# Flamingo block with a gated mixture of experts: group 0's first gates spread by TensorE, its weights split in three turns, group 1's second norm later, constant products in TensorE's waits

## The chip, the cores and the metric

The kernel runs on one core of a Trainium2 chip. The metric is the device time of a launch in microseconds; the runs of the kernel before gave 799.54, 800.27 and 800.44, median 800.27. Engines: TensorE (PE, its weight loads PEld), VectorE (DVE), ScalarE (ACT), GpSimd (POOL) and SyncE (SP), which issues nearly all DMAs. All times below are microseconds from the start of the profiled span unless marked ns.

## The reference

64 sequences of 128 tokens with 128 channels. Cut to what is computed:

```
x = x + tanh(g_xattn) * cross_attention(ctx, layernorm(x))        # 77 context tokens a sequence
h = layernorm(x)
logits = (h/|h|) @ (sim/|sim|) - sigmoid(gates)                   # 16 experts
w = softmax over active experts (those with logits > 0, or the top 2 if there is none)
q, k, v = sum_e w[:, e] * (h @ proj_m[e])       for m in q, k, v  # 16 experts each
o = softmax(q k^T / sqrt(128)) v                                  # within a sequence
x = x + tanh(g_ffn) * sum_e w[:, e] * (o @ o_proj[e])
```

## The kernel before

The 64 sequences are 16 groups of four, so a group has 512 tokens, one full row of a PSUM bank. TensorE's main work is a pass per group with 16 steps (experts). In `experts(i, s)` (L1380) expert s of group i adds its products to the three accumulators acc_q, acc_k, acc_v: for each of the three, high weights by high half of the data, low weights by high half, high weights by low half, nine matmuls of 128x512 in half precision. Each number is split in a high and a low float16 part so that the sum is nearly as exact as float32.

The data of a step are made by a chain over three engines: DVE multiplies the normalized tokens x2T_p by the gate of the expert, spread over all partitions (`zq_scale`, L1145, writes zq_full); ACT rounds this to float16 (`zq_high`, L743); POOL subtracts to get the low half (`zq_low`, L658). They run LEAD = 4 steps ahead of TensorE. The spread gates (wq_bc) come through DRAM: DVE transposes the gates to w_blk, SP writes them to w_rows and reads each row back to all 128 partitions (`weight_rows` L468, `spread_q` L476), two experts a transfer.

Beside a pass run, at fixed steps, the small stages of the neighbouring groups: cross attention of group i+2, second norm (`second_stats`, `second_rstd`, `x2_norm`) and gates (`gate_logits`, `gate_mask`, `gate_softmax`) of group i+1, attention and output products of group i-1 (`y_pair`, L1409). There is no scheduler: every engine's order is written out in its `head()` and in `body(i)`, which runs over the steps s, and semaphores join the engines. `late(i)` shifts the gate steps of pass 0.

The head does groups 0 and 1 up to their first norms and loads the projections into `stage`. The projections must be scaled to float16: `weight_max` (L1020) takes the largest entry of each, `gather_max` (L1366) and `spread_max` (L1371) bring it to all partitions through TensorE, `weight_scales` makes the factors, then `weight_high` (ACT, L737) and `weight_low` (DVE, L1068) split a whole projection of 2048 columns per instruction. For q, k, v this is in the head; o_proj follows in pass 0 (`MAX_AT`, `SHARE_AT`, `HIGH_AT`, `LOW_AT` name the steps). `first_expert` (L1396 to L1401) is expert 0 of group 0 in an order of its own. `keep_busy(n)` (L1560) is n matmuls of the identity by itself, whose result is never read.

## Time and profile before

| | us |
|---|---|
| median of three runs (lowest, highest) | 800.27 (799.54, 800.44) |
| profiled execution | 799.99 |
| its span | 798.1 |
| first expert's first matmul | 43.21 |
| start of expert 8 of pass 0 | 63.80 |
| TensorE busy in the span | 776.1 |

The span is what the rows are read from; 1.9 of the profiled execution's time lie around it. A busy TensorE is not TensorE at its peak: matmuls overlap, so what the start times of successive instructions say counts. A row of the timeline gives start, duration, engine, line, operation, the tile written and the tiles read, and in brackets the idle time before it with what ended it.

### The profile page before, as it was taken

Reading aid. Unit: us, or ns where it says so; the run is one execution under the profiler, and the core shown is the slowest. Engines: PE = TensorE matmul, PEld = TensorE weight load, DVE = VectorE, ACT = ScalarE, POOL = GpSimd, SP = SyncE. Lnnn points to the kernel's source line nnn. Section 1 sums busy time; section 2 is a strip of 40 time slices with the busy share of each in tenths; the row PEclk is TensorE's granted clock in tenths of the full one; section 3 lists DMA queues with packets and bytes.
Section 4 is the critical chain, followed back from the end, with each engine's and each line's share of the span. In section 5 each row is a group of like instructions: output and inputs, shape, how many; then the busy total and the mean of one; then the engine's idle time right before and its main releaser. Section 6 shows DMA issues by size and latency. Waiting matters only on the chain.

```text
span 798.1 us, 13995 instructions
## 1 busy us (share of the span) xinstructions
PE 776.1 (97%) x3999; PEld 418.1 (52%) x3999; DVE 607.2 (76%) x2037; ACT 433.8 (54%) x1129; POOL 483.0 (61%) x703
## 2 busy tenths in 40 slices
PE   7489999999999999999999999999999999999998
PEld 6445545555455555545555554555555455544444
DVE  2977787878787787778777787877878786775648
ACT  5554645556555655655565565456556555544445
POOL 3276657674746757474675747567574755765534
PEclk9789999999999999999999999999999999999999
DMA  6564476563655636365563636546364654543100
GB/s 192 136 216 159 162 219 174 169 209 94 209 161 164 189 106 204 97 210 167 151 191 106 202 109 209 166 150 186 101 207 116 208 160 139 163 135 116 53 14 28
DMA packets 97476, 122.57 MB, mean 154 GB/s; under 512 B 14611, under 2 KB 69111, under 8 KB 97399
## 3 DMA queue, kind: packets, MB, share of 16 engines
q1 hardware_dynamic: 96679, 121.59, 49.6%
q8 instruction: 32, 0.52, 0.3%
q14 instruction: 45, 0.37, 0.1%
q10 hardware_dynamic: 720, 0.08, 0.1%
HBM read 97.32 MB, written 24.31 MB: 152 GB/s over the span
## 4 chain that ended last, share of the span: by engine, by line
PE 88%; DVE 5%; DMA 2%; POOL 1%; ACT 1%; issue 1%; SPq 0%; DVEq 0%; ACTq 0%; POOLq 0%
PE acc_q L1380 20%; PE acc_k L1380 20%; PE acc_v L1380 20%; PE y L1409 9%; PE oT_p L1409 9%; PE m L1489 2%; PE m L1553 2%; DVE x_all L1175 1%; PE oT_p L1641 1%; PE m L1480 1%; PE m L1539 1%; DMA stage<-in_L_ffn_q_proj_dram 1%; PE m L1469 1%; POOL zq L658 1%; PE m L1529 1%
## 5 line engine op out<-in xcount | busy, mean ns | idle before, releaser
L658 POOL TENSOR_TENSOR zq<-zq_full,zq 128x512 f16<-128x512 f32 x256 | 297.8, 1170 | 222.4 <-ACT zq L743 222.2
L743 ACT ACTIVATE zq<-zq_full 128x512 f16<-128x512 f32 x256 | 160.1, 636 | 224.1 <-DVE zq_full L1145 224.0
L1175 DVE SCALAR_TENSOR_TENSOR x_all<-y,w_out,x_all 128x128 f32<-128x128 f32 x356 | 122.2, 343 | 96.1 <-issue 69.5
L1380 PE MATMUL acc_q<-zq,w_hi 128*128 128x512 f16 x510 | 193.3, 379 | 1.0 <-POOL zq L658 1.0
L1380 PE MATMUL acc_k<-zq,w_hi 128*128 128x512 f16 x510 | 193.2, 379 | 0.0
L1380 PE MATMUL acc_v<-zq,w_hi 128*128 128x512 f16 x510 | 193.2, 379 | 0.0
L1145 DVE TENSOR_TENSOR zq_full<-wq_bc,x2T_p 128x512 f32<-128x512 f32 x256 | 167.8, 668 | 2.5 <-DMA wq_bc<-w_rows 1.7
L1175 DVE SCALAR_TENSOR_TENSOR x_all<-oT_p,w_out,x_all 128x128 f32<-128x128 f32 x356 | 121.5, 341 | 0.0
L673 POOL TENSOR_TENSOR x_all<-stage,x_all 128x128 f32<-128x128 f32 x240 | 100.4, 456 | 19.8 <-DVE x_all L1175 13.3
L1380 PE MATMUL acc_q<-zq,w_lo 128*128 128x512 f16 x255 | 96.6, 379 | 0.0
L1380 PE MATMUL acc_v<-zq,w_lo 128*128 128x512 f16 x255 | 96.6, 379 | 0.0
L1380 PE MATMUL acc_k<-zq,w_lo 128*128 128x512 f16 x255 | 96.6, 379 | 0.0
L1409 PE MATMUL y<-w_hi,oT 128*128 128x512 f16 x236 | 89.5, 379 | 1.5 <-ACT oT L975 1.3
L1409 PE MATMUL oT_p<-w_hi,oT 128*128 128x512 f16 x236 | 89.4, 379 | 0.0
L1380 PEld LDWEIGHTS acc_v<-zq,w_hi 128*128 128x128 f16 x510 | 53.7, 105 | 53.3
L1380 PEld LDWEIGHTS acc_q<-zq,w_hi 128*128 128x128 f16 x510 | 51.8, 102 | 53.7 <-POOL zq L658 2.2
L1380 PEld LDWEIGHTS acc_k<-zq,w_hi 128*128 128x128 f16 x510 | 49.8, 98 | 53.3
L770 ACT ACTIVATE stage<-oT_p,w_out 128x128 f32<-128x128 f32 x116 | 33.1, 368 | 69.8 <-PE oT_p L1409 45.6
L1409 PE MATMUL oT_p<-w_lo,oT 128*128 128x512 f16 x118 | 44.7, 379 | 0.0
L1409 PE MATMUL y<-w_lo,oT 128*128 128x512 f16 x118 | 44.7, 379 | 0.0
L1380 PEld LDWEIGHTS acc_k<-zq,w_lo 128*128 128x128 f16 x255 | 26.8, 105 | 26.7
L1380 PEld LDWEIGHTS acc_v<-zq,w_lo 128*128 128x128 f16 x255 | 24.9, 98 | 26.7
(253 smaller groups left out, 1091.4 us busy)
## 6 DMA issues: line engine op xcount, KB each, us to landing
wq_bc<-w_rows SPq DMA_DIRECT2D x128, 512.0 KB, 4.5
blk_rows<-stage SPq DMA_DIRECT2D x26, 256.0 KB, 2.7
stage<-blk_rows SPq DMA_DIRECT2D x104, 64.0 KB, 2.0
blk_rows<-v_blk SPq DMA_DIRECT2D x15, 256.0 KB, 2.0
v_mix<-blk_rows SPq DMA_DIRECT2D x60, 64.0 KB, 2.9
blk_rows<-pc_blk SPq DMA_DIRECT2D x15, 256.0 KB, 4.1
pcT<-blk_rows SPq DMA_DIRECT2D x60, 64.0 KB, 2.0
out_dram<-x_all SPq DMA_DIRECT2D x15, 256.0 KB, 6.7
```

The costliest lines, as they stand in the source:

```text
L658: nc.gpsimd.tensor_tensor(zq[:, 1, e % Z_SLOTS, :], zq_full[:, e % F_SLOTS, :], zq[:, 0, e % Z_SLOTS, :], ALU.subtract).then_inc(zq_lo_poo ...
L673: nc.gpsimd.tensor_tensor(total, y_sc[:, n // 2 % 2, b, j, :], total, ALU.add).then_inc(y_pool_added, 1)
L743: nc.scalar.activation(zq[:, 0, e % Z_SLOTS, :], zq_full[:, e % F_SLOTS, :], ACT.Copy).then_inc(zq_hi_done, 1)
L770: last = nc.scalar.activation(dst, bank[:, tok(j)], ACT.Copy, scale=w_out[:, g % 2, e, b0 + b:b0 + b + 1])
L1145: nc.vector.tensor_tensor(zq_full[:, e % F_SLOTS, :], wq_bc[:, e // 2 % W_SLOTS, e % 2], x2T_p[:], ALU.mult).then_inc(zq_full_done, 1)
L1175: nc.vector.scalar_tensor_tensor(out=rows(x_all, g, b0 + b), in0=bank[:, tok(j)], scalar=w_out[:, g % 2, e, b0 + b:b0 + b + 1], in1=rows(x ...
L1380: last = nc.tensor.matmul(acc[m][:], w[:, m, s, :], zq[:, half, s % Z_SLOTS, :], start=(s == 0 and n == 0), stop=(s == E - 1 and n == 2))
L1409: last = nc.tensor.matmul(bank[:], oT[:, g % 2, half, tok(b)], w[:, O, QUAD * k:QUAD * (k + 1), :].rearrange("p e c -> p (e c)"), start=(n ...
L1469: last = nc.tensor.matmul(m0[:, b * E:(b + 1) * E], x2T[:, tok(b)], sn[:], start=True, stop=True)
L1480: last = nc.tensor.matmul(m1[:, b * S:(b + 1) * S], xnT[:, tok(b)], kxT[:, ctx_slot(g1), b * S:(b + 1) * S], start=True, stop=True)
L1489: done = nc.tensor.matmul(m1[:, tok(b)], qT[:, tok(b)], kT[:, tok(b)], start=True, stop=True)
L1553: last = nc.tensor.matmul(m1[:, tok(b)], pxT[:, tok(b)], vx[:, ctx_slot(g), tok(b)], start=True, stop=True)
```

## The change

1. **First gates by TensorE.** `gate_diagonal(e)` on DVE multiplies the identity by the gates of expert e, four times side by side (128x512, float32), and `gate_spread(e)` on TensorE multiplies a matrix of ones by it: every partition gets the gates of the 512 tokens, in PSUM. This is done for experts 0 and 1 of group 0 (`BY_PE = 2`); the products `zq_scale(0, 0)` and `(0, 1)` read PSUM and x2T, and SP's first transfer of that group's spread gates is left out.
2. **Weights in three turns.** `weight_high` and `weight_low` of q, k, v take a part each time, experts 0 to 3, 4 to 9, 10 to 15 (`PARTS`): the first in the head, the second in the head and at step 0, the third at steps 1 to 4 of pass 0. `experts` waits for the second part at step 4 and for the third at step 10.
3. **Order of the head and of pass 0.** The q projection is loaded before the extra context, x of group 1 before v; group 0's gates come before the weight scales; `att_product(1)`, `x1_add(1)`, `second_stats(1)`, `second_rstd(1)`, `x2_norm(1)` and `first_stats(2)` move from the head into pass 0; `GATES_LATE = 3` puts group 1's second norm and gates two steps later than before; the steps of o_proj's largest entry, its sharing, and its split are each one or two later.
4. **`oT_high(0)`** stands ahead of the step's `zq_high` in pass 1 instead of behind it.
5. **`keep_busy`** stands at ten more places of TensorE's head, before its waits.

```diff
+BY_PE = 2
+PARTS = ((0, 4), (4, 10), (10, 16))
+GATES_LATE = 3
-            return 1 if i == 0 else 0
+            return GATES_LATE if i == 0 else 0
-        MAX_AT, SHARE_AT = (0, 2), ((0, 4), (0, 7))
-        HIGH_AT = (0, 9)
-        LOW_AT = (0, 11)
+        MAX_AT, SHARE_AT = (0, 4), ((0, 5), (0, 8))
+        HIGH_AT = (0, 10)
+        LOW_AT = (0, 12)
...
                 sp.wait_ge(kq_in, 16 * 2)
+                load_weights(Q, q_proj)
                 sp.dma_start(zq_full[0:S, 0:PRE]...   # extra context
-                load_weights(Q, q_proj)
                 load_weights(K, k_proj)
+                load_x(1)
                 load_weights(V, v_proj)
-                load_x(1)
...
                 # POOL, pass 0
+                    if i == 0 and s == 2:
+                        second_rstd(1)
...
+                    if i == 0 and s == 3:
+                        first_rstd(2)
...
                 # ACT, pass 0 and 1
+                    if i == 1 and s == Y_FIRST:
+                        oT_high(0)
                     for g, e in zq_at(i, s):
                         zq_high(g, e)
...
+                    if i == 0 and s == 3:
+                        x2_norm(1)
+                    if i == 0 and s in (1, 2, 3):
+                        weight_high((Q, K, V)[s - 1], 2)
...
+            def gate_diagonal(e):
+                wait(dve, w_ready, 1)
+                nc.vector.tensor_tensor(wq_bc[:, 0, e].rearrange("p (b t) -> p b t", b=G),
+                                        ident[:].unsqueeze(1).broadcast_to([P, G, P]),
+                                        w_new[:, 0, e].unsqueeze(2).broadcast_to([P, G, P]),
+                                        ALU.mult).then_inc(w_diag_done, 1)
...
                 # DVE, head (tail of it)
+                gate_softmax(0)
+                gate_diagonal(0)
                 weight_scales(0)
+                gate_diagonal(1)
                 x_sum(1)
                 zq_scale(0, 0)
+                weight_low(Q)
                 zq_scale(0, 1)
+                weight_low(K)
                 weight_low(V)
+                weight_low(Q, 1)
                 zq_scale(0, 2)
                 zq_scale(0, 3)
+                weight_low(K, 1)
...
+                    if i == 0 and s == 0:
+                        weight_low(V, 1)
+                    if i == 0 and s == 1:
+                        x1_add(1)
+                        second_stats(1)
+                    if i == 0 and s == 2:
+                        first_stats(2)
+                    if i == 0 and s in (2, 3, 4):
+                        weight_low((Q, K, V)[s - 2], 2)
...
+            def gate_spread(e):
+                pe.wait_ge(w_diag_done, e + 1)
+                pe.wait_ge(logit_read, 1)
+                nc.tensor.matmul(SPREAD_BANKS[e][:], ones[:], wq_bc[:, 0, e], start=True,
+                                 stop=True).then_inc(w_spread_ps, 1)
...
                 # TensorE, end of the head
+                keep_busy(8)
+                gate_spread(0)
                 px_transpose(1)
-                att_product(1)
+                keep_busy(2)
+                gate_spread(1)
+                keep_busy(3)
```

TensorE around step 4 and 5 of pass 0. `m<-ident,x` is group 1's transposition after its second norm, `y<-ident,wmax` is `gather_max(1)` for o_proj, `m<-sn,x2T` are group 1's gate logits. Before:

```order
L1500 MATMUL m<-ident,x 128x128 x3
L1380 MATMUL acc_q<-zq,w_hi 128x512 [waits zq_lo_pool]
L1380 MATMUL acc_q<-zq,w_lo 128x512
L1380 MATMUL acc_q<-zq,w_hi 128x512
L1380 MATMUL acc_k<-zq,w_hi 128x512
L1380 MATMUL acc_k<-zq,w_lo 128x512
L1380 MATMUL acc_k<-zq,w_hi 128x512
L1380 MATMUL acc_v<-zq,w_hi 128x512
L1380 MATMUL acc_v<-zq,w_lo 128x512
L1380 MATMUL acc_v<-zq,w_hi 128x512
L1366 MATMUL y<-ident,wmax 4x128 [waits prep_dve,wmax_done]
```

and with the change:

```order
L1439 MATMUL acc_v<-zq,w_hi 128x512
L1561 MATMUL m<-ident,x 128x128 [waits xnT_sb,zq_full_done,logit_read,x2_done]
L1561 MATMUL m<-ident,x 128x128 x3
L1421 MATMUL y<-ident,wmax 4x128 [waits prep_dve,wmax_done]
L1439 MATMUL acc_q<-zq,w_hi 128x512 [waits zq_lo_pool]
```

Both now stand between experts 5 and 6; they were behind experts 3 and 4, a whole expert between them.

DVE around `weight_max(O)`, which is `wmax<-stage`, the instruction that `gather_max(1)` waits for. Before, its neighbours are the products of experts 6 and 7:

```order
L1007 BN_AGGR mv<-bn 128x2 x3
L1145 TENSOR_TENSOR zq_full<-wq_bc,x2T_p 128x512 [waits zq_lo_pool,wq_in2]
L1145 TENSOR_TENSOR zq_full<-wq_bc,x2T_p 128x512 [waits zq_lo_pool]
L1145 TENSOR_TENSOR zq_full<-wq_bc,x2T_p 128x512 [waits zq_lo_pool,wq_in3]
L1020 TENSOR_REDUCE wmax<-stage 128x1 [waits proj_in3]
```

and with the change, where w_lo are the third parts for q, k and v:

```order
L1037 BN_AGGR mv<-bn 128x2 x3
L1098 SCALAR_TENSOR_TENSOR w_lo<-stage,w_up,w_hi 128x768 [waits hi_done0]
L1190 TENSOR_TENSOR zq_full<-wq_bc,x2T_p 128x512 [waits zq_lo_pool]
L1098 SCALAR_TENSOR_TENSOR w_lo<-stage,w_up,w_hi 128x768 [waits hi_done1]
L1190 TENSOR_TENSOR zq_full<-wq_bc,x2T_p 128x512 [waits zq_lo_pool,wq_in0]
L1098 SCALAR_TENSOR_TENSOR w_lo<-stage,w_up,w_hi 128x768 [waits hi_done2]
L1020 TENSOR_REDUCE wmax<-stage 128x1 [waits proj_in3]
```

It stood behind seven products (experts 0 to 6) and now stands behind nine, and behind three more pieces of the weights.

ACT in pass 1 at step 8. Before:

```order
L820 ACTIVATE gate_e<-gate_arg 128x64 [waits gate_arg_done]
L743 ACTIVATE zq<-zq_full 128x512 [waits zq_used,zq_full_done] x3
L975 ACTIVATE oT<-oT_p 128x512 [waits oT_ps]
L850 ACTIVATE px,sum_x<-m,nmax_x 128x77 [waits rsum_x_done,pxT_ps,xmax_done]
```

and with the change:

```order
L837 ACTIVATE gate_e<-gate_arg 128x64 [waits gate_arg_done]
L760 ACTIVATE zq<-zq_full 128x512 [waits zq_used,zq_full_done] x2
L899 ACTIVATE oT<-oT_p 128x512 [waits oT_ps]
L760 ACTIVATE zq<-zq_full 128x512 [waits zq_used,zq_full_done]
L867 ACTIVATE px,sum_x<-m,nmax_x 128x77 [waits rsum_x_done,pxT_ps,xmax_done]
```

The rounding of group 0's attention output (oT) goes one product forward.

## Rows read from the trace of the kernel before

**Rows 1.** The page: busy time of each engine, with its share and instructions.
```profile
PE 776.1 (97%) x3999; PEld 418.1 (52%) x3999; DVE 607.2 (76%) x2037; ACT 433.8 (54%) x1129; POOL 483.0 (61%) x703
```

**Rows 2.** TensorE's waits from 57 to the end: total, times, longest.
```profile
PE y L1409 <- ACT oT L975: 1.3, 2, 1.0
```

**Rows 3.** Stretches: length, busy PE, PEld, DVE, ACT, POOL, PEclk, DMA share, GB/s.
```profile
28.00:32.90 4.90, 0.00 (x0) 0.00 (x0) 4.35 (x34) 3.56 (x6) 1.71 (x4) 0.57 0.04 11
43.20:46.90 3.70, 3.53 (x9) 0.88 (x9) 3.67 (x8) 0.90 (x2) 3.70 (x2) 0.65 0.66 264
54.43:63.80 9.37, 9.37 (x51) 5.11 (x51) 7.04 (x25) 4.84 (x11) 7.78 (x9) 1.00 0.53 170
102.55:103.74 1.19, 0.16 (x1) 0.03 (x1) 0.11 (x1) 1.19 (x4) 0.97 (x2) 1.00 1.05 278
```

**Rows 4.** Timeline, TensorE, pass 0 and 1.
```profile
56.38 0.27 PE L1366 MATMUL y<-ident,wmax 128*4 128x128 f32 x1
63.80 0.39 PE L1380 MATMUL acc_q<-zq,w_hi 128*128 128x512 f16 x1
...
100.60 0.38 PE L1380 MATMUL acc_q<-zq,w_hi 128*128 128x512 f16 x1
102.33 0.38 PE L1380 MATMUL acc_v<-zq,w_hi 128*128 128x512 f16 x1
103.74 0.38 PE L1409 MATMUL y<-w_hi,oT 128*128 128x512 f16 x1 [1.03 <-ACT oT L975]
104.38 0.39 PE L1409 MATMUL y<-w_hi,oT 128*128 128x512 f16 x1
```

**Rows 5.** Timeline, DVE, from group 0's gates to o_proj's largest entry.
```profile
34.33 2.31 DVE L1068 SCALAR_TENSOR_TENSOR w_lo<-stage,w_up,w_hi 128x2048 f16<-128x2048 f32 x1
...
41.36 1.28 DVE L1145 TENSOR_TENSOR zq_full<-wq_bc,x2T_p 128x512 f32<-128x512 f32 x2 [1.71 <-DMA wq_bc<-w_rows]
...
45.42 1.12 DVE L1218 SCALAR_TENSOR_TENSOR x_all<-m,rsum_x,x_all 128x128 f32<-128x128 f32 x4
...
47.78 0.65 DVE L1145 TENSOR_TENSOR zq_full<-wq_bc,x2T_p 128x512 f32<-128x512 f32 x1
...
51.31 2.28 DVE L1020 TENSOR_REDUCE wmax<-stage 128x1 f32<-128x2048 f32 x1
```

**Rows 6.** Timeline, DVE and POOL, where both want SBUF at once.
```profile
29.88 0.23 DVE L1088 TENSOR_TENSOR logit<-logit,sig 128x64 f32<-128x64 f32 x1
...
43.03 5.11 POOL L658 TENSOR_TENSOR zq<-zq_full,zq 128x512 f16<-128x512 f32 x3 [12.47 <-ACT zq L743]
...
57.15 4.51 POOL L658 TENSOR_TENSOR zq<-zq_full,zq 128x512 f16<-128x512 f32 x4
...
59.38 1.23 DVE L1088 TENSOR_TENSOR logit<-logit,sig 128x64 f32<-128x64 f32 x1
```

**Rows 7.** Timeline, ACT.
```profile
40.45 1.99 ACT L737 ACTIVATE w_hi<-stage,w_up 128x2048 f16<-128x2048 f32 x1
...
51.36 1.63 ACT L781 ACTIVATE x<-x_all,shift,rstd 128x128 f32<-128x128 f32 x4
...
102.48 0.63 ACT L743 ACTIVATE zq<-zq_full 128x512 f16<-128x512 f32 x1 [0.75 <-DVE zq_full L1145]
103.02 0.58 ACT L975 ACTIVATE oT<-oT_p 128x512 f16<-128x512 f32 x1
```

**Rows 8.** Timeline, POOL: first and last instruction of `second_rstd(1)` and of `second_norm(1)`.
```profile
48.23 0.23 POOL L641 TENSOR_SCALAR shift<-mv 128x4 f32<-128x4 f32 x1
...
49.95 0.20 POOL L646 TENSOR_TENSOR shift<-shift,rstd 128x4 f32<-128x4 f32 x1
...
55.58 0.23 POOL L650 TENSOR_SCALAR norm<-mv 128x4 f32<-128x4 f32 x1
...
57.00 0.20 POOL L654 TENSOR_TENSOR norm<-norm,rstd 128x4 f32<-128x4 f32 x1
```

**Rows 9.** Timeline, TensorE: a float32 matmul of 308 columns in the head.
```profile
18.66 0.69 PE L1529 MATMUL y<-ctxT,m_kq 128*128 128x308 f32 x2
```

More of the change, by code:

```diff
@@ L411, in vx_bank, with split_part @@
             return (acc[V], oT_p, acc[K])[g - 1] if 1 <= g <= PRE else m0
+        SPREAD_BANKS = (m0, oT_p)
+        def split_part(t, m, part):
+            experts = slice(*PARTS[part]) if m < O else slice(0, E)
+            return t[:, m, experts].rearrange("p e h -> p (e h)")
         def ctx_slot(g):
@@ L507, in head @@
                 weight_rows(0)
-                for j in range(W_SLOTS):
+                for j in range(BY_PE // 2, W_SLOTS):
                     spread_q(0, j)
@@ L682, in head @@
                 first_rstd(1)
-                for e in range(LEAD - 1):
+                for e in range(LEAD):
                     zq_low(0, e)
-                second_rstd(1)
-                zq_low(0, LEAD - 1)
-                first_rstd(2)
             def body(i):
@@ L877, in pxT_out, with oT_high @@
                                          px_mix[:].rearrange("p i b n -> p b i n"), ACT.Copy).then_inc(pxT_sb, 1)
+            def oT_high(g):
+                wait(act, oT_ps, g + 1)
+                wait(act, y_ps, PAIRS_Y * (g - 1))
+                nc.scalar.activation(oT[:, g % 2, 0, :], oT_p[:], ACT.Copy).then_inc(oT_hi_done, 1)
             def head():
@@ L904, in head @@
                 xnT_out(1)
-                x2T_move(0)
+                x_exps(1)
+                weight_high(Q)
                 weight_high(K)
-                x_exps(1)
+                zq_high(0, 0)
+                weight_high(V)
                 pxT_out(1)
-                weight_high(V)
-                for e in range(LEAD):
-                    zq_high(0, e)
+                zq_high(0, 1)
+                weight_high(Q, 1)
+                weight_high(K, 1)
+                zq_high(0, 2)
+                weight_high(V, 1)
+                zq_high(0, 3)
             def body(i):
@@ L932, in body @@
                         y_scale(gd, 7, banks=(0,))
-                    if s == (3 if i == 0 else 0) and has(g1):
+                    if s == (4 if i == 0 else 0) and has(g1):
                         x_norm(g1)
@@ L971, in body @@
                         kxT_out(g1)
-                    if s == Y_FIRST and has(gc):
-                        wait(act, oT_ps, gc + 1)
-                        wait(act, y_ps, PAIRS_Y * (gc - 1))
-                        nc.scalar.activation(oT[:, gc % 2, 0, :], oT_p[:], ACT.Copy).then_inc(oT_hi_done, 1)
+                    if s == Y_FIRST and i > 1 and has(gc):
+                        oT_high(gc)
                     if s == 10 - sooner(i) and has(g1):
@@ L1376, in experts @@
                 for m in (Q, K, V):
+                    for part, (first, _) in enumerate(PARTS):
+                        if (i, s) == (0, first):
+                            pe.wait_ge(hi_done[m], part + 1)
+                            pe.wait_ge(lo_done[m], part + 1)
                     if s == 0:
@@ L1506, in xn_transpose @@
                     wait(pe, kxT_sb, 2)
-                wait(pe, logit_read, cap(g))
+                if g == 2:
+                    wait(pe, x1_done, 2)
                 for b in range(G):
-                    last = nc.tensor.transpose((acc[Q] if g == 1 else m0)[:, tok(b)], xn[:, b, :], ident[:])
+                    last = nc.tensor.transpose((m0, acc[Q], m1)[g][:, tok(b)], xn[:, b, :], ident[:])
                 last.then_inc(xnT_ps, 1)
@@ L1574, in head @@
                 vx_product(0)
-                for g in range(1, PRE + 1):
-                    ctx_transpose(g)
-                px_transpose(0)
-                kx_product(1)
-                att_product(0)
-                vx_product(1)
-                for g in range(2, PRE + 1):
+                ctx_transpose(1)
+                px_transpose(0)
+                for g in range(2, PRE + 1):
+                    ctx_transpose(g)
+                att_product(0)
+                for g in range(1, PRE + 1):
                     kx_product(g)
@@ L1618, in body @@
                         scores(gc, i)
+                    if i == 0 and s == 0:
+                        att_product(1)
                     if s == 2 + late(i) and g2 < X2_HEAD:
```

77 lines of the change are left out of this document (43 added, 34 removed).

## Prediction

> **What bounds the kernel now.** I read the page's busy times first: TensorE is busy for 776.1 of 798.1 [rows 1]. Then TensorE's waits: from 57 on there is one of weight, 1.3 before the first output products, of which 1.0 in one piece [rows 2]. So the end is set by how early TensorE gets into its unbroken stream and by that one wait; nothing else in 740 us is for sale. Third, stretches: from 54.43 TensorE is busy all of 9.37 at clock 1.00 (2.4 GHz), while it stood still from 28.0 to 32.9 and did the first expert at a mean clock of 0.65, that is, mostly at 1.2 GHz [rows 3]. Last the timelines, for what each wait in pass 0 hangs on.
>
> I measure the change at one mark: the start of expert 8 of pass 0, 63.80 before [rows 4]. Behind it both kernels have the same work left but for one small matmul (`spread_max(1)`, now behind expert 8), 0.1. All times are on the scale of the profiled execution; its time is 799.99, 0.28 under the median of the runs shown.
>
> **The change part by part: the front of the head.** Loads are reordered. The q projection starts earlier, but the extra context now comes behind it, and group 0's score transposition stands behind a transposition that waits for that context. DVE loses the weight scales (moved behind the gates) and gains group 1's row maxima ahead of w_blk, the point at which DVE began the low weights, 34.33 [rows 5]. I add these up to w_blk at 34.0; the order of the two loads could make it one earlier or nearly one later.
>
> **First products.** From 34.0 on DVE does a diagonal (512 columns, like a product, which has 1.28/2 = 0.64 [rows 5]), the scales (five operations of under 0.23 [rows 6], 0.85), a second diagonal, and a short reciprocal: 36.2. The spread is a float32 matmul of 512 columns, which the trace doesn't have; from 0.69 for 308 columns [rows 9] it is 1.15 by columns, under that if a fixed part is in it, and twice that if the clock is at half: 1.0 to 2.3, and I take 1.0, since the constant products now fill the waits. The first spread is hidden under the scales; the second ends at 37.6, so the products of experts 0 and 1 start at 36.2 and 37.6, where they started at 41.4 and 42.0, behind a transfer [rows 5]. Expert 2 still needs that transfer: 41.36 - 34.33 = 7.0 after w_blk, 41.0.
>
> **First experts.** The first part of the weights is 512 columns: ACT 1.99/4 = 0.5 and a little [rows 7], DVE 2.31/4 = 0.6 and a little [rows 5]; I take 0.5 and 0.65, and 0.75 and 0.9 for 768 columns. TensorE starts its first expert at 38.2 instead of 43.2. An expert is 1.94: eight steps from 100.60 to 102.33 make 0.216, times nine [rows 4]. With `att_product(1)` (0.9) and waits of 1.8 for the third low part and 0.4 and less for products 2 and 3, experts 4 and 5 run from 49.2 to 53.1. In the kernel before, expert 4 began at 54.43 [rows 3]. Up to here 5 us are won.
>
> **What takes them back.** Behind expert 5 stand two waits. `x2_transpose(1)` needs the second norm of group 1: DVE does `x1_add(1)` and its statistics (45.42 to 47.78, 2.35 [rows 5]) at 46.7 to 49.1, POOL's reciprocal root takes 48.23 to 50.15, 1.9 [rows 8], so 51.3, and ACT's norm 1.63 [rows 7] stands behind the product of expert 7: 53.0 to 54.7. The transposition ends at 55.1. Then `gather_max(1)` needs the largest entry of o_proj, and that is DVE's backlog. Its work from 34.0 to that point: diagonals 1.3, scales 0.85, nine products at 0.62, 5.6, the low weights in three pieces of 0.65 and six of 0.9, 7.4, `x1_add` and its statistics 2.35, the first statistics of group 2 another 1.2, the maximum 2.2 [rows 5], small ones 0.1: 20.9, so 54.9 if DVE never waits. The kernel before was done at 53.59, with two products less, larger pieces and no diagonals.
>
> It will wait. DVE's operations with both inputs in SBUF and POOL's subtractions exclude each other here: 64 columns take 0.23 on a free POOL and 1.23 beside subtractions, and POOL's three subtractions at 43.03 take 5.11, where four take 4.51 at 57.15, because a low weight was running [rows 6]. In the kernel before only the last low weight met a subtraction. Now eight of the nine pieces come after POOL has begun. Placing them one by one, DVE waits 0.35 at k's first piece, 1.05 at v's, 0.45 at v's second, 0.4 at k's third; and 1.1 at v's third, whose high half stands on ACT behind the second norm (54.7). With 0.4 for the second spread that is 3.75: 58.7. The bounds are no wait for POOL, 2.3 less, and a whole subtraction (4.51/4 = 1.13 [rows 6]) at each of the eight, 5 more than I take.
>
> This is where a page speaks: the Trainium skill, SBUF — State Buffer, section "Who interferes with whom", says that a VectorE instruction with two SBUF inputs and a GpSimd one that reads SBUF take a shared port for the whole instruction, whichever comes first. The rows agree. By it the low weights in small pieces cost no less port time, only more meetings.
>
> So expert 6 starts at 58.85, expert 7 behind the transposition of group 2's norm (0.44), with the logits in it (0.5), and expert 8 at 63.7; before it was 63.80. A second chain ends at nearly the same place, so that a quicker DVE alone doesn't help much: POOL does `second_norm(1)` (55.58 to 57.20, 1.6 [rows 8]) and then `first_rstd(2)` (1.9) ahead of ACT's norm of group 2, which ends at 60.0, and TensorE needs that before expert 7, at 60.8. With the matmul still to do the head is worth 0.0, the 5 us gone into the wait at `gather_max(1)`.
>
> **Pass 1.** The wait before the first output products goes: TensorE is ready at 102.33 + 0.22 = 102.55 and starts at 103.74, busy for 0.16 of the 1.19 between [rows 3]; the third product waits again until 104.38, 0.21 late [rows 4]. ACT did the product of expert 12 first (102.48), then oT, 0.58 [rows 7]. Turned round, oT starts after the product before, at 101.7, and is in time. Next late is `oT_low` on DVE, still behind its product: it would end at 103.1 to 103.4 and hold the third matmul for up to 0.4. Gain 1.19 + 0.21 - 0.4 = 1.0.
>
> **Others.** Group 1's gates now follow on the logits in expert 7, so that they come two steps nearer to their use. From 63.8 DVE has some 25 small operations of 0.23 and less [rows 6] and two products, 5.7, so 69.5; 7.0 for the way through DRAM as for group 0, 76.5; then product, rounding and subtraction, 2.4, with `weight_low(O)` in between, 2.3 by the first low weight [rows 5]: 81.2. TensorE needs it at 63.8 plus eight experts and 2.1 of small matmuls, 81.4. So this is only just hidden, and each us that the gates slip further costs up to 1. The constant products lie in waits: nothing. The second and third weight waits at steps 4 and 10 are met 3 and more earlier.
>
> Sum: 799.99 - 0.0 - 1.0 = 799.0.
>
> **The rivals.**
> - *An earlier, looser head* (faster). The q load lands sooner and carries DVE's chain with it by 1.0, which reaches the mark whole, since both waits behind expert 5 hang on it; port waits half as long give 0.5 more. 799.0 - 1.5 = 797.5. For it: the mark moves one for one with w_blk. Against it: the context behind the q load.
> - *The clock falls in the new wait* (no change). TensorE stands from 55.1 to 58.8, 3.7, after another 1.6. In a stop of 4.9 the clock was at half for most of it and stayed so into the first experts [rows 3]. Half of 2.7 us of experts at half speed is 1.35: 800.35. Decides if the stop stays over some 3. The Trainium skill, TensorE: Matmul & The Clock Gate, section "Why this matters for your kernels", warns of idle gaps between bursts for this reason; the constant products stand in the head alone, not here.
> - *The spreads run at half clock* (slower; also: the constant products don't do what they say). Then the second spread ends at 40.6, as group 1's transposition and the constant products ahead of it are slow too; the second product is 3.0 late, of which DVE's later waits absorb 1.2. The rest, 1.8, reaches `gather_max(1)`, and the clock is lost there as well: 799.0 + 1.8 + 1.35 = 802.15. It decides from w_blk plus 4.5 for the second product. For it: clock 0.57 from 28.0 to 32.9 [rows 3]. Against it: the waits there are now filled.
>
> **How the numbers follow.** Forecast 0.42, earlier head 0.25, clock in the wait 0.19, half-clock spreads 0.14. The forecast's own range is 798.2 to 799.9. 0.2% is 1.6, about what a measurement of this kernel can tell from no change: faster is under 798.7, slower over 801.9. Faster: all but a little of the second case and a third of the forecast's, 0.24 + 0.14 = 0.38. Slower: most of the last and the tail of the third, 0.13. Same 0.49. The range 796.6 to 802.0 leaves out one tenth on either side: below, w_blk one earlier and no port waits; above, the last case.
>
> **What would show it.** w_blk near 34.0; the first product before 37 and the first expert near 38; low weights of 128x768 that last 1.0 and more instead of 0.9; TensorE idle for about 3.7 before `y<-ident,wmax`, ended by DVE's maximum at 58.7; PEclk 1.00 from 28 to 55; expert 8 near 63.7; no wait on oT in pass 1. It is wrong if the matmul of o_proj's maximum doesn't wait, which would mean that DVE isn't behind (then expert 8 comes up to 1 earlier), or if TensorE waits at the first expert of pass 1 for its low half.

## The result and the profile after

The changed kernel took 807.45 us (median of 4 runs, 806.79 to 808.93), the kernel before 800.36 (4 runs, 799.54 to 800.63): ratio 1.0093, 95% interval 1.0075 to 1.0110. It is slower by 7.1; the forecast was 799.0, with 802.0 as the range's upper end. The profiled run was the slowest of the four, 808.93 with a span of 807.1 against 798.1 before, so the traces have 9.0 to explain, 1.9 more than the medians. From the page of the changed kernel, the lines that answer to [rows 1]:

```profile
PE 784.2 (97%) x4055; PEld 424.3 (53%) x4055; DVE 609.4 (76%) x2045; ACT 434.2 (54%) x1135; POOL 483.9 (60%) x703
...
PE   5979989999999999999999999999999999999998
...
PEclk9998999999999999999999999999999999999999
...
PE 86%; DVE 6%; DMA 4%; issue 1%; ACT 1%; SPq 1%; DVEq 0%; ACTq 0%
```

TensorE is busy 8.1 longer with the constant products in it, and the chain of work that ended last now passes more through transfers (DMA 4%, where the kernel before has 2%). Which ones, its list of waits says (what it waited for, total, times, longest), against [rows 2]:

```profile
PE y L1582 <- DMA zq_full<-in_ctx_dram: 3.7, 1, 3.7
PE y L1421 <- DVE wmax L1050: 3.4, 1, 3.4
...
PE oT_p L1721 <- DMA pcT<-blk_rows: 2.9, 1, 2.9
PE acc_q L1439 <- POOL zq L674: 1.5, 2, 1.1
...
PE y L1469 <- ACT oT L899: 0.3, 1, 0.3
```

Three pieces of 2.9 and more: the first (context) and the third (the transposed probabilities of pass 1) were not there before, the second is the wait that the prediction placed. The same list shows the wait on oT down from 1.3 to 0.3. The first in TensorE's timeline (start, duration):

```profile
16.58 0.49 PE L1582 MATMUL y<-ident,zq_full 77*128 77x77 f32 x4 [3.67 <-DMA zq_full<-in_ctx_dram]
...
18.72 2.00 PE L1615 MATMUL m<-vx,pxT 77*128 77x128 f32 x8
```

The eight matrix products at 18.72 take 2.00, where they took 1.16 before: behind the stop TensorE runs at 1.2 GHz. They are group 0's cross attention, which VectorE adds to x on the way to the gates:

```profile
20.75 1.13 DVE L1263 SCALAR_TENSOR_TENSOR x_all<-m,rsum_x,x_all 128x128 f32<-128x128 f32 x4 [4.53 <-PE m L1615]
```

In the kernel before this sum began at 19.02. Stretches of the changed kernel (length, busy, granted clock), three stops and what followed each:

```profile
12.90:16.60 3.70, 0.03 (x2) 1.00 1.08 276
16.60:22.00 5.40, 5.40 (x29) 0.53 0.98 281
28.00:32.90 4.90, 4.77 (x42) 1.00 0.12 32
...
57.20:60.66 3.46, 0.04 (x1) 0.61 0.88 272
60.66:64.90 4.24, 4.24 (x12) 0.52 0.07 22
...
105.40:108.36 2.96, 0.02 (x2) 1.00 0.34 89
108.36:112.50 4.14, 4.14 (x16) 0.59 1.01 294
```

After each of these three stops some 4 to 5 us are at about half (0.52 to 0.59); from 28.0 to 32.9, where the kernel before stood still at 0.57 [rows 3], the clock is full. VectorE's timeline gives the second stop and what stands behind group 1's gates:

```profile
57.40 1.02 DVE L1098 SCALAR_TENSOR_TENSOR w_lo<-stage,w_up,w_hi 128x768 f16<-128x768 f32 x1 [1.08 <-ACT w_hi L754]
58.33 2.28 DVE L1050 TENSOR_REDUCE wmax<-stage 128x1 f32<-128x2048 f32 x1
...
73.75 0.24 DVE L1170 STREAM_TRANSPOSE w_blk<-w_new 128x64 f32<-128x64 f32 x1
...
81.69 0.69 DVE L1190 TENSOR_TENSOR zq_full<-wq_bc,x2T_p 128x512 f32<-128x512 f32 x1 [3.77 <-DMA wq_bc<-w_rows]
82.29 2.34 DVE L1098 SCALAR_TENSOR_TENSOR w_lo<-stage,w_up,w_hi 128x2048 f16<-128x2048 f32 x1
...
91.46 0.71 DVE L1111 STREAM_TRANSPOSE stage<-xn 128x512 f32<-128x512 f32 x1 [1.04 <-ACT xn L821]
```

VectorE stands for 3.77 on the transfer of group 1's gates, and only then does the low half of o_proj and all that leads to group 3's norm, whose block is ready at 92.2. That is 1.2 behind the scores (91.01), where it was 0.8 behind them before (86.12 and 85.28). SyncE's queue in pass 1, of the changed kernel:

```profile
92.20 0.32 SPq L471 DMA_DIRECT2D blk_rows<-stage  x1
...
97.44 2.68 SPq L477 DMA_DIRECT2D stage<-blk_rows  x4
100.17 0.43 SPq L492 DMA_DIRECT2D wq_bc<-w_rows  x1
100.64 0.43 SPq L471 DMA_DIRECT2D blk_rows<-pc_blk  x1
```

and of the kernel before:

```profile
86.12 0.32 SPq L455 DMA_DIRECT2D blk_rows<-stage  x1
...
89.37 1.73 SPq L461 DMA_DIRECT2D stage<-blk_rows  x4
91.14 0.43 SPq L476 DMA_DIRECT2D wq_bc<-w_rows  x1
92.54 0.34 SPq L455 DMA_DIRECT2D blk_rows<-pc_blk  x1
```

In this kernel SyncE waits until a block has landed in DRAM before it fetches it back (the four transfers from blk_rows), and what stands behind that wait in its order stands too. Before, the probabilities' block left as soon as it was ready. Now the norm's block takes 5.2 from issue to landing instead of 3.2, and the probabilities, ready at 98.3, leave at 100.64. TensorE, in the changed kernel:

```profile
108.36 1.34 PE L1721 MATMUL oT_p<-pcT,v_sb 128*128 128x128 f32 x8 [2.94 <-DMA pcT<-blk_rows]
109.49 0.63 PE L1439 MATMUL acc_q<-zq,w_hi 128*128 128x512 f16 x1
...
112.95 0.38 PE L1469 MATMUL y<-w_hi,oT 128*128 128x512 f16 x1
```

The first output product follows its expert at once, so that the wait of [rows 4] is gone, but most of the expert ran at half clock (a product every 0.43 instead of 0.22).

The whole difference, by five marks of the timelines, one profiled execution of each kernel. The rows below the second are the experiments of the next section. The marks: the first w_blk on VectorE; group 2's score transposition on TensorE (behind expert 12 of pass 0); the scores of pass 1; the oT product; the first output product.

| | w_blk | to transp. | to scores | to oT | to output | to end |
|---|---|---|---|---|---|---|
| before | 34.16 | 40.08 | 11.04 | 14.36 | 4.10 | 694.36 |
| changed | 36.35 | 42.13 | 12.53 | 17.35 | 4.59 | 694.15 |
| a1 context first | 33.01 | 41.83 | 12.44 | 16.87 | 4.59 | 694.16 |
| a2 busy gather | 36.85 | 40.15 | 12.91 | 15.49 | 2.91 | 694.19 |
| a3 gather later | 37.80 | 42.64 | 12.22 | 16.78 | 4.52 | 694.24 |
| a4 low half earlier | 37.38 | 42.16 | 12.13 | 15.22 | 2.91 | 694.20 |
| b1 = a1 + a2 | 33.23 | 40.13 | 12.71 | 15.52 | 2.91 | 694.20 |
| b2 = b1 + a4 | 33.50 | 40.14 | 12.12 | 14.92 | 2.91 | 694.21 |
| b3 gates earlier | 33.09 | 42.87 | 11.04 | 14.97 | 2.91 | 694.12 |
| b4 before, oT first | 33.82 | 40.01 | 11.04 | 14.43 | 2.91 | 694.29 |
| c1 gather later, filled | 33.84 | 40.46 | 11.50 | 14.79 | 2.91 | 694.20 |
| c2 pxT first | 33.78 | 40.16 | 11.61 | 15.12 | 2.91 | 694.22 |
| c3 three chains | 33.87 | 38.65 | 11.05 | 15.98 | 2.91 | 694.14 |
| c4 no constants | 34.32 | 41.83 | 12.13 | 14.36 | 2.91 | 694.15 |
| d1 block order | 36.29 | 42.19 | 12.80 | 14.81 | 2.91 | 694.20 |
| d2 = c3 + d1 | 33.67 | 38.66 | 11.05 | 14.65 | 2.91 | 694.16 |
| d3 = c3, gates earlier | 33.04 | 39.62 | 11.04 | 15.95 | 2.91 | 694.24 |

Changed less before, column by column: 2.19 + 2.05 + 1.49 + 2.99 + 0.49 - 0.21 = 9.0. The first column moves from run to run (the five kernels with the q load first lie at 36.3 to 37.8, the ten others with a diagonal at 33.0 to 34.3). So a median and a column of the table can tell different amounts, and where they do, both are given. The second, fifth and last column repeat to about 0.1, the two between to about 0.5, since transfers are in them.

### The profile page after: what moved, and what is told of

Same layout as the page of the kernel before. It is cut to its first block, busy times and chain, and to the rows that moved or that the text cites. A ratio compares the mean times of both kernels' runs of the same rounds, so it can differ in the third digit from the quotient of the medians.

```text
span 807.1 us, 14130 instructions
## 1 busy us (share of the span) xinstructions
PE 784.2 (97%) x4055; PEld 424.3 (53%) x4055; DVE 609.4 (76%) x2045; ACT 434.2 (54%) x1135; POOL 483.9 (60%) x703
## 4 chain that ended last, share of the span: by engine, by line
PE 86%; DVE 6%; DMA 4%; issue 1%; ACT 1%; SPq 1%; DVEq 0%; ACTq 0%
PE acc_k L1439 19%; PE acc_q L1439 19%; PE acc_v L1439 19%; PE oT_p L1469 9%; PE y L1469 9%; PE m L1549 2%; PE m L1615 2%; PE oT_p L1721 2%; DVE x_all L1220 1%; PE m L1601 1%; PE m L1540 1%; DVE zq_full L1190 1%; DMA zq_full<-in_ctx_dram 1%; PE m L1529 1%; PE m L1591 1%
```

## The experiments

**a1**, the load order alone.

```diff
-                load_weights(Q, q_proj)
                 sp.dma_start(zq_full[0:S, 0:PRE]..., c_v[:, G:G * (PRE + 1), :])...
+                load_weights(Q, q_proj)
```

> The changed kernel with one thing undone: the extra context is loaded ahead of the q projection again, as in the kernel before. Theory A: the late head is a late context. TensorE's wait of 3.7 for it (12.9 to 16.6) goes, and with it the half-speed stretch behind it; the first w_blk comes at 34.0 to 34.5 instead of 36.4 (by the end of the softmax on VectorE), expert 8 of pass 0 at 65.4 to 65.7 instead of 67.64, and all that follows is 2.0 to 2.3 earlier: about 805.3 as a median against 807.4. Rival B: the path to w_blk goes over the q projection's maximum on VectorE; then w_blk stays at 36 or comes later, and the time stays at 807.4 or rises.

Measured 804.71 (5 runs, 802.57 to 806.05; ratio to before 1.0048, 1.0029 to 1.0066), 2.7 under the changed kernel. w_blk comes 3.3 earlier, at 33.01; no later column moves by over 0.5. Theory A, and in the trace more than it said. VectorE in a1:

```profile
16.02 2.29 DVE L1049 TENSOR_REDUCE wmax<-stage 128x1 f32<-128x2048 f32 x1 [2.11 <-DMA stage<-in_L_ffn_q_proj_dram]
...
18.50 1.13 DVE L1262 SCALAR_TENSOR_TENSOR x_all<-m,rsum_x,x_all 128x128 f32<-128x128 f32 x4
```

Here the sum that TensorE held up until 20.75 in the changed kernel comes at 18.50, right behind the q projection's maximum, which had waited for its load. So rival B named a path that is real, but only once the context is in time: with the q load first the way to w_blk goes over the context and TensorE, with the context first over the q load and its maximum.

**a2**, constant products in the wait at the gather.

```diff
                     if (i, s) == SHARE_AT[0]:
+                        keep_busy(12)
                         gather_max(1, y0)
```

> The changed kernel with twelve constant products of 128 columns (about 0.22 each, 2.6 in all) ahead of the transposition of the weights' maxima in pass 0, in TensorE's wait of 3.4. Theory A: the clock falls to half because TensorE stands there, and that costs 1.9 of its own: expert 6 begins at 60.9 as now, but the experts behind it run at 1.94 instead of 3.85, expert 8 comes at 65.7 to 66.0 instead of 67.64, and the time is 1.7 to 1.9 less, about 805.6. Rival B: another engine sets the pace behind the wait (the norm of group 2 on ScalarE ends at 62.0, so expert 7 cannot begin before 62.5), and at most 0.5 comes back. Rival C: the gates of group 1 and the transfers behind them set the time in pass 1, and the gain in pass 0 is lost there.

Measured 806.37 (4 runs, 804.26 to 807.55; ratio 1.0081, 1.0064 to 1.0098). That is 1.1 under the changed kernel, less than theory A's 1.7 to 1.9, and the two intervals overlap: the time alone doesn't settle it. The profiled run is the fastest of the four, so what it shows in pass 1 need not be typical. In the trace:

```profile
57.60 2.84 PE L1629 MATMUL y<-ident 128*128 128x128 f32 x24
61.18 0.27 PE L1421 MATMUL y<-ident,wmax 128*4 128x128 f32 x1 [0.74 <-DVE wmax L1050]
```

VectorE's maximum ends where it did against w_blk, expert 6 takes 1.94 instead of 3.84, and the second column is 40.15 instead of 42.13: the clock is worth 2.0 in that column. b1 against a1, the same edit with ten runs, has 1.7 there. Theory A by the trace; B falls, the norm of group 2 is in time for this. Rival C said that pass 1 would take the gain back; b1, below, speaks against it.

**a3**, the gather moved away from the wait.

```diff
-        MAX_AT, SHARE_AT = (0, 4), ((0, 5), (0, 8))
+        MAX_AT, SHARE_AT = (0, 4), ((0, 7), (0, 9))
```

> The changed kernel with the transposition of the weights' maxima moved from behind expert 5 to behind expert 7, and their spread from behind expert 8 to behind expert 9. Theory A (the second chain of the prediction): TensorE starts expert 6 at 57.2 instead of 60.9, but then waits at the transposition of group 2's norm until the norm ends at 62.0, some 2.9, so that only 2 to 3 are won: expert 8 at 64.9 to 65.7, time about 805. Rival B: VectorE's maximum was the only wait; all of 3.4 and the clock's 1.9 come back, expert 8 at 62.4, time about 802.

Measured 807.66 (4 runs, 806.35 to 809.99; the slowest was profiled): nothing won, both expectations too good. TensorE's row, with the wait in brackets:

```profile
63.53 1.12 PE L1571 MATMUL m<-ident,xn 128*128 128x128 f32 x4 [2.89 <-ACT xn L821]
```

The second chain is there, 2.9 of wait in the place of 3.4. The transposition comes 2.6 sooner behind w_blk than in the changed kernel (25.7 against 28.3), but the clock falls as well (0.63 from 63.5 to 72.0) and takes it all back: 42.64.

**a4**, the low half of o_proj in VectorE's wait.

```diff
-        LOW_AT = (0, 12)
+        LOW_AT = (0, 11)
```

> The changed kernel with the low half of o_proj (2.3 on VectorE) moved ahead of the first product of pass 1, into VectorE's wait of 3.8 for the transfer of group 1's gates. Theory A: the low half behind that wait holds up VectorE's queue, ScalarE's and then the transfers: the wait of 0.45 at the first expert of pass 1 goes, the block of group 3's norm leaves 2.1 earlier (90.1 instead of 92.2), so that the probabilities' block no longer stands behind it in the transfer queue (issued by 98 instead of 100.64), TensorE's wait of 2.9 for the transposed probabilities goes and the clock stays full: 4 to 5 less, about 802.8. Rival B: the transfer of the gates itself (74.0 to 81.6) sets pass 1, and the low half only fills a gap: at most 0.6 less, about 806.8.

Measured 805.41 (4 runs, 805.00 to 806.02; ratio 1.0063). Scores to oT 15.22 instead of 17.35, the stop before oT 0.8 instead of 2.9, and the clock holds: 2.91 instead of 4.59. In those columns that is 3.8; the medians differ by 2.0, under A's 4 to 5 and over B's 0.6; w_blk was 1.0 later in that run. Only the place of VectorE's piece was changed, but A's way to the gain is not what the trace shows: the norm's block leaves at 92.51, 0.8 behind the scores instead of 1.2, so 0.4 sooner and not 2.1, and it is fetched 3.2 behind its issue instead of 5.2. Most of the column's gain is that shorter transfer, and why it was shorter stays open (below).

**b1** and **b2**, the edits together (a1 + a2, and a4 on top).

> The changed kernel with the extra context ahead of the q load (a1) and the twelve constant products ahead of the transposition of the maxima (a2). Theory A: the two are independent terms, the late context about 2.7 and the clock about 2.0 at the mark (the first part of group 2's score transposition in TensorE's row came 40.15 behind w_blk with the products, 41.83 to 42.13 without). So that transposition comes 40.2 behind w_blk, level with the kernel before (40.08), and the time is 801.5 to 803.5, still above 800.4 by what the late gates cost in pass 1. Rival B: the waits in pass 1 hang on transfers that started at fixed times, and the two gains do not add: 804.7 as a1.

> b1 with the low half of o_proj ahead of the first product of pass 1 (a4's edit). Theory A: VectorE's queue behind the transfer of the gates is the third term; alone it gave 2.0. Scores to oT product in pass 1: 15.2 instead of about 16.9, and the stop before oT under 1, so that the clock holds; the time is 1.5 to 3 under b1, 799.5 to 801.0. Rival B: b1 has ended the long stop already (with the clock), and this gives at most 0.5.

Measured: b1 800.69 (10 runs, 800.37 to 801.71; ratio 1.0006, 0.9997 to 1.0016), b2 799.53 (10 runs; 0.9988, 0.9979 to 0.9998). b1 is 6.8 under the changed kernel, better than theory A: the stop before oT is down to 1.1 and the clock holds there too. Against a1, the constant products are worth 4.0 in the medians, 1.7 of it in pass 0 and the rest in the shorter stop and the kept clock of pass 1; no run here tells why that stop is shorter with them. b2 has another 1.2, less than A's 1.5 and more than B's 0.5. What is left of the two waits in pass 1 that come from group 1's gates, in b2's list of waits:

```profile
PE m L1614 <- ACT pxT L889: 0.8, 1, 0.8
...
PE oT_p L1720 <- DMA pcT<-blk_rows: 0.5, 1, 0.5
```

**b3**, group 1's gates one expert earlier, on b2.

```diff
-GATES_LATE = 3
+GATES_LATE = 2
...
+                    if i == 0 and s == 2 + late(i):
+                        x2T_out(g2)
                     if s == (4 if i == 0 else 0) and has(g1):
                         x_norm(g1)
...
```

> b2 with group 1's transposition, logits and gates one expert earlier in pass 0 (two behind the kernel before's instead of two and one more: logits in expert 6), and ScalarE's copy of the transposed norm ahead of group 2's norm, since expert 6 needs it. Theory A: the late gates are what is left. The second w_blk comes about 1.5 to 2 earlier, VectorE's wait for the transfer falls from 3.8 to 2 or less, the wait at the attention product of group 2 (0.5 to 1.0, behind the same transfer through ScalarE's queue) goes, and pass 1 has no wait for the transposed probabilities: 1 to 2 under b2, 798.0 to 799.5, under the kernel before. Rival B: VectorE is behind in pass 0 anyway (its maximum of o_proj), so that the gates do not start earlier by more than 0.5 and nothing is won.

Measured 801.56 (10 runs; ratio 1.0016, 1.0003 to 1.0030), 2.0 over b2: neither theory.

```profile
53.34 0.66 PE L1562 MATMUL m<-ident,x 128*128 128x128 f32 x4 [3.24 <-ACT x L797]
...
53.30:60.00 6.70, 6.66 (x36) 0.75 0.57 173
```

The transposition waits 3.2 for a norm that is no earlier against w_blk, and the clock falls for expert 5. But to the scores it takes 11.04, as in the kernel before.

**b4**, the kernel before with the oT move alone.

```diff
+                    if i == 1 and s == Y_FIRST:
+                        oT_high(0)
                     for g, e in zq_at(i, s):
                         zq_high(g, e)
...
```

> The kernel before with one part of the change alone: in pass 1 ScalarE rounds oT ahead of its next rounding of a product. The prediction priced this at 1.0 less. Theory A: the trace of the changed kernel shows the whole wait gone, 1.19 before the first output product, and the third product's 0.21, with no wait at the low half: 1.4 less, 799.0. Rival B: the low half on VectorE is late and holds TensorE at the third product for up to 0.4: 1.0 less, 799.4. Rival C: the product whose rounding is put off delays the next experts: no gain.

Measured 798.92 (10 runs; ratio 0.9985, 0.9976 to 0.9995): 1.3 less. The interval holds both A's 1.4 and B's 1.0; the trace decides for theory A.

```profile
102.21 0.38 PE L1414 MATMUL y<-w_hi,oT 128*128 128x512 f16 x1
...
102.70 0.39 PE L1414 MATMUL y<-w_hi,oT 128*128 128x512 f16 x1
```

The first follows its expert at once, and the third is 0.06 late, where the prediction allowed up to 0.4.

**c1**, **c2**, **c3**, what lies behind the gather, all on b2's edits (c1 and c3 with the constants ahead of group 2's transposition instead of the gather, twelve in c1 and five in c3).

```diff
 c1:
-        MAX_AT, SHARE_AT = (0, 4), ((0, 5), (0, 8))
+        MAX_AT, SHARE_AT = (0, 4), ((0, 7), (0, 9))
 c2, ahead of ScalarE's rounding in step 12:
+                    if i == 0 and s == 12:
+                        pxT_out(g1)
...
 c3, both of these, and on GpSimd:
+                    if i == 0 and s == 3:
+                        first_rstd(2)
                     if s == (3 if i == 0 else 1) and i < 2:
                         second_norm(g2)
 and on ScalarE:
+                    if i == 0 and s == 4:
+                        x2T_out(g2)
                     if s == (4 if i == 0 else 0) and has(g1):
                         x_norm(g1)
...
```

> b2 with the maxima's transposition behind expert 7 (a3's move), and the twelve constant products now ahead of group 2's transposition instead. Theory A: the wait at the gather hides a second wait of nearly the same end, ScalarE's norm of group 2, so that with the clock held the move is worth only 0.6 to 1.0: that transposition comes 25.7 behind w_blk (26.4 in b2), and the time is 798.5 to 799.0. In a3 the same move lost all of it, since the wait of 2.9 was unfilled and the clock fell. Rival B: the norm waits for something that the maximum holds up as well, and nothing is won (799.5).

> b2 with ScalarE's copy of group 2's transposed probabilities ahead of its first rounding of pass 1, which waits for the transfer of group 1's gates. Theory A: TensorE's wait of 0.8 at the attention product of group 2 is that transfer, seen through ScalarE's queue: it goes, and what is late next is the first expert of pass 1, whose gates come with the same transfer: of the 0.8, 0.2 to 0.8 is won, 798.7 to 799.3. Rival B: the first expert of pass 1 waits for the same transfer and takes it all: 799.5.

> c1 and c2 together, with the two other things that hold expert 7: GpSimd takes group 2's reciprocal root ahead of group 1's norm, and ScalarE copies group 1's transposed norm ahead of group 2's norm (five constant products ahead of group 2's transposition). Theory A: three chains end within 2 of each other behind expert 5 (the maximum on VectorE, the norm of group 2 through GpSimd and ScalarE, the copy behind a rounding that waits for VectorE). With all three moved the transposition of group 2 comes 24.0 to 24.7 behind w_blk instead of 26.4, and the time is 1.5 to 2.5 under b2: 797.0 to 798.0, under both kernels. Rival B: a fourth, the roundings and subtractions of experts 8 to 10 behind VectorE's maximum, takes it back: 798.5 to 799.5.

Measured: c1 799.01 (10 runs, 798.17 to 800.82; ratio 0.9985), c2 799.45 (10 runs; 0.9987), c3 797.66 (6 runs, 796.31 to 798.43; ratio 0.9961, 0.9948 to 0.9973). Group 2's transposition comes 25.8 behind w_blk in c1, as said, but 0.5 is lost again in a wait of the spread, the second column is no shorter than b2's, and the medians of the two can't be told apart. c2 takes 0.5 out of the third column, and the median is b2's: too little to tell, rival B as far as one sees. c3 is the one that counts. GpSimd, ScalarE and TensorE in it:

```profile
56.06 0.20 POOL L651 TENSOR_TENSOR shift<-shift,rstd 128x4 f32<-128x4 f32 x1
...
56.30 1.65 ACT L820 ACTIVATE xn<-x_all,shift,rstd 128x128 f32<-128x128 f32 x4 [0.41 <-POOL shift L651]
...
57.99 0.66 PE L1574 MATMUL m<-ident,xn 128*128 128x128 f32 x4 [0.17 <-ACT xn L820]
```

The transposition comes 24.1 behind w_blk and waits for 0.2 only; the second column falls to 38.65, 1.4 under the kernel before. Theory A; how much each of the moved pieces gives was not measured. Its fourth column is 1.1 longer than b2's: the block of the norm took 5.1 there, the probabilities stood behind it on SyncE, and TensorE waited 1.4 for them.

**c4**, b2 without the constant products that the change put into the head. They are eight calls with 26 products (4, 2, 3, 2, 2, 8, 2 and 3). The edit of the first is shown. The expectation's 32 is a miscount, and so are the ten more places that the description of the change names: the changed kernel has ten calls, two of which were there before.

```diff
                 x2_transpose(0)
-                keep_busy(4)
                 pe.wait_ge(vx_sb, PRE)
...
```

> b2 without the eight calls that the change added to the head between group 0's norm and the first expert (32 constant products); those ahead of them and the twelve before the gather stay. Theory A (the rival of the prediction that did not happen): without them the clock falls between w_blk and the first experts as in the kernel before (0.57 from 28 to 33): the spreads take 2.0 each instead of 1.0, the first expert comes 1 to 1.5 later and runs at half speed; VectorE's backlog absorbs most, and the time is 0.5 to 2.5 over b2: 800 to 802. Rival B: TensorE's waits there are short enough without them, or VectorE's backlog absorbs all: 799.5.

Measured 801.78 (10 runs, 800.09 to 803.11; ratio 1.0016, 1.0006 to 1.0025): 2.25 over b2, theory A.

```profile
35.20 2.07 PE L1622 MATMUL m<-wq_bc,ones 128*128 128x512 f32 x2 [2.39 <-DVE wq_bc L1104]
...
37.91 1.92 PE L1622 MATMUL oT_p<-wq_bc,ones 128*128 128x512 f32 x2
...
33.00:37.00 4.00, 1.80 (x2) 0.75 (x3) 3.37 (x14) 2.37 (x10) 0.00 (x0) 0.50 0.06 8
```

At clock 0.50 the spreads take 2.0 each instead of 1.0, w_blk is 0.8 later and the first expert another 1.1.

**d1** and **d2**, SyncE's order in pass 1, on the changed kernel and on c3.

```diff
+                    if s == 3 and i == 1:
+                        wait(sp, pc_blk_done, gc + 1)
+                        blocks_out(2, pc_blk, pc_blk_out)
                     if s == 3 and X_HEAD <= g1 < NG:
                         wait(sp, xn_blk_out, 16 * (g1 - X_HEAD + 1))
...
```

> The changed kernel with one thing moved: in pass 1 SyncE sends the block of group 0's probabilities ahead of fetching the transposed block of group 3's norm, for which it waits 4.6 and spends 2.7 on the issue; nothing is removed. Theory A: TensorE's wait of 2.9 for the transposed probabilities is queueing on SyncE, which lets the block go at 100.64 though it was ready at 98.2: the block leaves 2.4 earlier relative to the scores, the wait falls to 0.5 or so and the clock's 1.7 behind it comes back: 803 to 804.5 against 807.45. Rival B: the transfers themselves are slow there (4.3 for the block, beside the broadcasts of the gates), and the order wins at most 0.5.

> c3 with the same order on SyncE. In c3 the block leaves at 91.73 and was ready at 90.4, and TensorE waits 1.4. Theory A: 1.2 of it goes: 796.2 to 796.8. Rival B (transfers): no change, 797.7.

Measured d1 804.97 (4 runs, 804.67 to 805.91; ratio 1.0060), d2 796.84 (4 runs, 795.49 to 797.87; ratio 0.9954, 0.9938 to 0.9971). SyncE in d1:

```profile
98.57 0.34 SPq L471 DMA_DIRECT2D blk_rows<-pc_blk  x1
99.00 1.82 SPq L477 DMA_DIRECT2D stage<-blk_rows  x4
100.87 0.43 SPq L492 DMA_DIRECT2D wq_bc<-w_rows  x1
101.34 1.85 SPq L477 DMA_DIRECT2D pcT<-blk_rows  x4
```

The probabilities' block leaves when ready and is fetched 2.8 later instead of 4.3, and TensorE waits 0.3 for it instead of 2.9: scores to oT 14.81 instead of 17.35, to the output 2.91 instead of 4.59. Against A's 803 to 804.5 the median is half a microsecond high; B, 0.5 at most, falls. The block also landed sooner once it had left (2.1 instead of 4.3), now ahead of the 512 KB broadcast of wq_bc and no longer behind it, so the order won both the queueing and a quicker transfer, and d1 doesn't part the two. d2's fourth column falls by 1.3, the median by 0.8, with an interval that overlaps c3's. Its median is the lowest of all, 3.3 under the 800.14 of the kernel before that was measured with it, but only the trace sets it apart from c3.

**d3**, b3's question again, on c3 with the wait filled.

```diff
-GATES_LATE = 3
+GATES_LATE = 2
...
+                        if i == 0:
+                            keep_busy(12)
                         x2_transpose(g2)
```

> c3 with group 1's transposition and logits one expert earlier, this time with twelve constant products in the wait ahead of the transposition, so that the clock cannot fall there as it may have in b3. Theory A: the lateness of the gates is itself a term in pass 1, and in b3 it was hidden by the clock: the second w_blk comes 1.5 to 2 earlier (32.0 to 32.5 behind the first, where c3 has 33.98), the wait for the transposed probabilities falls under 0.5, 796 to 797. Rival B: the wait at the earlier transposition (3.2) only moves expert 5, VectorE's products behind it come later, the second w_blk stays at about 34 behind the first and nothing is won or up to 1 is lost.

Measured 798.55 (10 runs; ratio 0.9982): 0.9 over c3. The second w_blk does come 32.4 behind the first (33.98 in c3), but the fourth column stays at 15.95 and the second is 1.0 longer. So with the three chains moved the place of the gates costs nothing more. c3 says the same: its second w_blk comes 4.7 ahead of group 2's score transposition, as in the changed kernel (before: 7.4), and still its third column is the 11.0 of the kernel before. What costs in the fourth column there is the order on SyncE (d2). Theory A had the w_blk right and the time wrong, B the time and not the w_blk.

## Why the prediction was wrong

Most steps of pass 0 came out, measured against w_blk: first expert 4.2 behind it (predicted 4.2), expert 4 14.9 (15.2), o_proj's maximum done 24.3 (24.7), VectorE's wait for v's third part 1.08 (1.1), a spread 1.0 (1.0). With the late context and the clock taken away (b1, b2) the second column is 40.1 against 40.1 before: "the head is worth 0.0" holds, the 5 us are lost at the gather as said, and a3 and c3 show that the second chain was real. The oT move was sized at 1.0 and measured 1.3 (b4); the 0.4 held back for the low half was too much. One bound was added up wrongly without effect: eight whole subtractions of 1.13 instead of the 3.35 of waits taken at those pieces are 5.7 more, not 5. What failed:

- **"I add these up to w_blk at 34.0"**: 36.35, 2.2 late. The text named the context behind the q load and allowed "nearly one". TensorE stood 3.7 for it and then worked at half clock, which the sum had not counted. The early q load did what the first rival said, its maximum began at 13.9 instead of 16.5, but VectorE then stood 4.5 for TensorE. With the order undone w_blk is at 33.0 (a1): the order costs 3.3 in the traces and 2.7 in the medians. Of the 3.3, 2.25 are VectorE's sum (20.75 against 18.50). Most of the rest is in TensorE's order: group 0's transposition for the gates, at 28.09, stood behind late matmuls and the eight constant products that both kernels have there, and began 2.5 behind the start of its norm, 1.7 in a1. Without this order w_blk lies at 33.0 to 34.3, against the 34.0 of the sum.
- **"The clock falls in the new wait"** was a rival at 0.19, priced at 1.35. It happened, at 2.0 (a2; 1.7 from a1 to b1). [Rows 3] showed a stop and a half-speed stretch behind it; this wait was predicted at 3.7 and nothing in the rows said that it was short enough.
- **"this is only just hidden, and each us that the gates slip further costs up to 1."** This is the step that failed worst. Against expert 8, w_blk came 0.6 later than forecast, and the transfer took 7.7 instead of 7.0. At the consumer that the sum had followed, the first expert of pass 1, TensorE waited no more than 0.4 for the low half. Yet pass 1 lost 1.49 + 2.99 and then 1.68 of clock (4.59 against 2.91), 6.2 in all, a term that the sum had at nothing. It did not name what is queued behind VectorE's waiting product: the low half of o_proj, ScalarE's copies (the wait at group 2's attention product), group 3's norm, and behind that norm's block, on SyncE, the probabilities. With a4's piece moved the fourth column is 2.1 shorter, with d1's one transfer 2.5; each also brings back the clock's 1.7. The two overlap, so their shares are not additive. Of this way the last part, on SyncE, is shown (d1). The first part, that VectorE's wait makes the norm's block late, accounts for 0.4 of the fourth column only; the 2.0 by which that block took longer to land is not explained by it.

What stays open: why the norm's block was fetched 3.0 to 3.5 behind its issue in some runs (before, a4, b2, b3, b4, c1, c4) and 4.1 to 5.2 behind it in others (changed, a1, a2, a3, b1, c2, c3, d3; d1 and d2 fetch it later by their order). The broadcasts of the gates are in flight beside it in all of them; no run here isolates it.

## What to carry to other kernels

When a step is made later, follow every queue behind the instruction that will wait, and not only the consumer that the step was made for. Here the consumer waited 0.4, and a stop of 2.9 stood elsewhere: a block that was ready, behind SyncE's wait for another one. When loads are reordered, ask the same of the one that now comes second. A stop of TensorE of 2.4 or more between experts was each time followed by some 4 us at half speed, so that its price was the stop and another 1.7 to 2.0; where the wait can't be removed, constant products in it gave that part back.

## What the runs showed of the hardware

- In pass 1, stops of 2.4 to 2.9 ahead of the oT product (changed, a1, a3) were followed by half clock and 4.5 to 4.6 to the output product; stops of 1.5 and less (all others) by full clock, and then 2.91 where oT is rounded first.
- The length of the stop alone doesn't decide. In the head, ahead of group 0's transposition, b1, b2, c1, c2 and d2 stopped for 2.5 to 3.0 and stayed at clock 1.00 for the next 6 us, their constant products following at once. c4, which leaves these out, stopped for 2.2, had further gaps of 0.8 and 0.4, and went on at 0.70 and then 0.50. c1's stop:

```profile
25.51 0.66 PE L1560 MATMUL m<-ident,x 128*128 128x128 f32 x4 [2.98 <-ACT x L797]
```

- Constant products at full rate in a stop kept the clock at 1.00 (a2: 57.7 to 65.4); 26 of them in the head were worth 2.25 (c4).
- One 462 KB load behind a 1 MB one instead of ahead of it made the first gates 3.3 later (changed against a1).
- One 256 KB block, written to DRAM in pass 1 beside broadcasts of 512 KB, took 3.0 to 5.2 from issue to fetch, and another one 2.1 (d1) and 4.3 (changed) to land.
